# Summing each window of nodes in PSUM, with the bank named by a register, in a four-layer graph network kernel

## The reference

```
# layer 0, twice (a and b): 4 bases, 8 edge types
m   = sum_b comp[etypes][:, b, None] * (h @ basis[b])[src] * norm[:, None]
agg = segment_sum(m, dst);  out = agg + bias + h @ loop_w
# layer 1: 8 bases, 32 edge types, the same without loop_w
# layer 2: deg = number of edges of dst, at least 1
ah  = segment_sum(x[src], dst) / deg[:, None];  out = x @ W1.T + b1 + ah @ W2.T + b2
# layer 3: attention over the same edges, 4 blocks of 4 heads
```

## Time and profile before

| | |
|---|---|
| median of 3 runs | 3148.48 us (3147.07 to 3153.4) |
| the profiled execution | 3150.06 us; its span 3148.7 us |
| L0a: steps, then turn | 47.65 to 326.8, then to 346.0 us |
| transform of L0a | to about 501 us |
| L0b: steps with turns | 514.1 to about 778 us (rows landed at 505.5) |
| L1: steps with turns | 906.8 to about 1203 us |
| layer 2 up to layer 3 | 1439 to about 1535 us |
| busy over the span | PE 94%, DVE 66%, ACT 40%, POOL 37% |

### The profile page before, as it was taken

How to read it: one execution, slowest core, us unless ns; L and a number is a source line. 1 busy time by engine, 2 the same in 40 slices (tenths; PEclk the granted TensorE clock), 3 DMA queues, 4 the chain that set the end, 5 groups by cost and what they waited for, 6 DMA issues and landing times.

```text
span 3148.7 us, 43883 instructions
## 1 busy us (share of the span) xinstructions
PE 2973.9 (94%) x14658; PEld 2178.0 (69%) x14658; DVE 2078.8 (66%) x5077; ACT 1274.5 (40%) x2245; POOL 1175.2 (37%) x938
## 2 busy tenths in 40 slices
PE   6899998999979899999999999999999999999999
PEld 3333775445843357875458998789987999779987
DVE  6999324886358853345377678567766776767777
ACT  4666531002340033342264454345543555435554
POOL 4666336665456643342012123511135101431022
PEclk8999999999989999999999999999999999999999
DMA  2555534555246643333013001210013001130012
GB/s 79 164 165 163 165 97 134 170 170 152 74 126 178 178 114 94 96 99 127 10 43 91 14 31 50 97 48 8 31 56 124 14 8 64 44 103 15 8 64 80
DMA packets 129600, 279.37 MB, mean 89 GB/s; under 512 B 22743, under 2 KB 45591, under 8 KB 128355
## 3 DMA queue, kind: packets, MB, share of 16 engines
q0 software_dynamic: 40320, 132.15, 14.6%
q1 hardware_dynamic: 87618, 141.76, 14.2%
q10 hardware_dynamic: 1440, 2.62, 0.2%
HBM read 227.85 MB, written 27.48 MB: 81 GB/s over the span
## 4 chain that ended last, share of the span: by engine, by line
PE 74%; DVE 12%; issue 9%; ACT 2%; DMA 2%; POOL 1%; DVEq 0%; another core or an unknown queue 0%; SPq 0%; POOLq 0%; ACTq 0%
PE bank L162 16%; PE bank L163 15%; PE bank L164 15%; PE bank L893 11%; PE bank L2548 5%; PE bank L2212 3%; PE bank L1853 2%; PE bank L861 2%; DVE y_tile L2164 1%; DVE y_tile L2166 1%; DVE columns L2147 1%; DVE G L1000 1%; DVE onehot_dst L967 1%; PE bank L907 1%; DMA yT_lo<-yT_new_lo 1%
## 5 line engine op out<-in xcount | busy, mean ns | idle before, releaser
L893 PE MATMUL bank<-gathered,selector 128*128 x1328 | 650.8, 614 | 57.6 <-SPq L849 32.0
L1000 DVE TENSOR_TENSOR G<-G,bank 128x512 f32 x664 | 453.7, 683 | 20.5 <-PE bank L893 20.0
L893 PEld LDWEIGHTS bank<-gathered,selector 128*128 128x128 f32 x1328 | 233.8, 194 | 312.8 <-issue 176.3
L2636 ACT CAST probT<-bank 128x512 fp32r<-128x512 f32 (+2 forms) x480 | 212.1, 516 | 261.8 <-PE bank L2548 260.9
L1514 POOL TENSOR_TENSOR weight_parts<-weight_ring,weight_parts 128x512 fp32r<-128x512 f32 x130 | 187.7, 1444 | 294.1 <-ACT weight_parts L1447 294.0
L2718 DVE CUSTOM_DVE_ANT_0 prob<-bank,count_by_src 128x512 f32<-128x512 f32 (+1 forms) x480 | 258.3, 588 | 58.8 <-PE bank L164 58.8
L1473 DVE TENSOR_TENSOR lhs_parts<-G,lhs_parts 128x640 fp32r<-128x640 f32 x122 | 102.3, 839 | 285.4 <-ACT lhs_parts L1445 285.2
L2644 DVE TENSOR_TENSOR probT<-bank,probT 128x512 fp32r<-128x512 f32 (+2 forms) x480 | 254.2, 585 | 50.8 <-ACT probT L2636 50.2
L871 ACT COPY G<-bank 128x512 f32<-128x512 f32 x160 | 82.4, 659 | 496.2 <-issue 250.7
L162 PE MATMUL bank<-weight_parts,lhs_parts 128*128 128x512 f32 x680 | 267.4, 393 | 11.1 <-POOL weight_parts L1514 5.6
L164 PE MATMUL bank<-weight_parts,lhs_parts 128*128 128x512 f32 x680 | 265.4, 390 | 0.0
(11 more groups left out here) (293 smaller groups left out, 6813.5 us busy)
## 6 DMA issues: line engine op xcount, KB each, us to landing
weight_ring<-in_L_gnn_basis SPq DMA_DIRECT2D x64, 256.0 KB, 2.6
weight_ring<-in_L_gnn_bases SPq DMA_DIRECT2D x64, 256.0 KB, 2.6
x_L<-x_rows SPq DMA_DIRECT2D x50, 256.0 KB, 4.3
x_rows<-x_L SPq DMA_DIRECT2D x50, 256.0 KB, 5.5
yT_hi<-yT_new_hi SPq DMA_DIRECT2D x4, 2560.0 KB, 11.3
yT_lo<-yT_new_lo SPq DMA_DIRECT2D x4, 2560.0 KB
count_rows<-count SPq DMA_DIRECT2D x10, 642.0 KB, 5.5
count_by_dst<-count_rows SPq DMA_DIRECT2D x10, 642.0 KB, 4.4
```

The costliest lines, as they stand in the source:

```text
L893: ins = pe.matmul(bank[s % banks][:], sel[:, s % SELECTORS, :], tile_rows_of[s % BATCH], start=True, stop=True)
L1000: ins = dve.tensor_tensor(g, g, bank[s % banks][:], ALU.add)
L2636: ins = act.copy(hi, of)
```

## The change

**In the steps.** A window now has a PSUM bank of its own, number (w + 1) % 4 for window w, and TensorE adds up all the window's steps in it (`start=False`), the bank named by a register. ScalarE clears four banks at the start; then, for each window, it waits for the window's last step (its number is in a new table, `end_of_window`), copies the bank into G once and clears it for the window four further on. VectorE only makes selectors; before each it waits until the bank of the step's window is cleared. G isn't cleared any more, and has no row for dropped steps. TensorE's register batch has twelve values, and more addresses.

**Counting.** Each step has one bf16 product of two one-hots, 128 rows (4 * node + high) by 320 (low), which adds up in banks 4 to 7 in the same way. VectorE makes both one-hots (L939, fp16 to bf16). ScalarE copies and clears 320 columns more for each window. The signs, PATHC and the halving go; layer 2 sums a row of counts (`sum_row`) for the degree where it formed the difference, and a row load now waits for that sum and for TensorE's transposes of the row four before.

**Around them.** Takes between steps are VectorE's; those behind the last step are ScalarE's and VectorE's in turn. The memset before L0b and L1 and the clearing at the start are gone. The setup makes `end_of_window`, bank numbers and the split of `src` and `dst` numbers in place of PATHC's tables.

The core of the diff (`aggregate`):

```diff
     def on_pool():
-        if free:
-            for token in free:
-                pool.wait_ge(*token)
-            pool.memset(G[:, 0:cleared, :], 0.0).then_inc(*zeroed_pool.inc())
         if counting:
             for t in range(RING):
                 gather(t)
         for token in ready:
             pool.wait_ge(*token)
-        if counting:
-            for first in range(0, counting.first, CLEARED):
-                pool.memset(G[:, first:min(first + CLEARED, counting.first), :], 0.0).then_inc(*zeroed_pool.inc())
...
     def on_pe():
         for token in ready:
             pe.wait_ge(*token)
-        tile_rows_of, tiles = batch(0)
+        tiles, rows_of, sums, counts = batch(0)
         for s in range(steps):
+            pe.wait_ge(*selected(s + 1))
+            if counting:
+                pe.matmul(counts[s % BATCH], counting.rows[:, s % SELECTORS, :], counting.sources[:, s % SELECTORS, :],
+                          start=False, stop=False, skip_group_check=True)
             pe.wait_ge(tiles_landed.semaphore.sem, tiles[s % BATCH])
-            pe.wait_ge(*selected(s + 1))
-            ins = pe.matmul(bank[s % banks][:], sel[:, s % SELECTORS, :], tile_rows_of[s % BATCH], start=True, stop=True)
-            if s >= banks:
-                ins._wait_ge(*added(s - banks + 1))
-            ins.then_inc(*multiplied.inc())
+            pe.matmul(sums[s % BATCH], sel[:, s % SELECTORS, :], rows_of[s % BATCH], start=False, stop=False,
+                      skip_group_check=True).then_inc(*multiplied.inc())
...
+        for w in range(windows):
+            b = sum_bank(w)
+            if w % BATCH == 0:
+                over = [v & COUNTED for v in table(C.end_of_window[path][0:1, w:w + BATCH], ACTE, 1, steps)]
+            act.wait_ge(multiplied.semaphore.sem, over[w % BATCH])
+            act.copy(G[:, w, :], psum[:, b, :]).then_inc(*summed.inc())
+            if counting:
+                act.copy(counting.count[:, w, :], psum[:, SUM_BANKS + b, 0:LOW]).then_inc(*counted.inc())
+            if w + SUM_BANKS < windows:
+                act.wait_ge(*summed(w + 1))
+                ins = act.copy(psum[:, b, :], C.zero[:].to_broadcast([P, D]))
+                if counting:
+                    act.wait_ge(*counted(w + 1))
+                    ins = act.copy(psum[:, SUM_BANKS + b, 0:LOW], C.zero[:].to_broadcast([P, LOW]))
+                ins.then_inc(*cleared.inc())
+        for n in range(NT * KC):
+            if taker[n] is act:
+                take(n, act)
+
+    def select(s, window):
+        at = s % SELECTORS
+        if s >= SELECTORS:
+            dve.wait_ge(*multiplied(s - SELECTORS + 1))
         if counting:
+            for onehot, numbers, place in ((counting.rows, counting.numbers[:, 0:P], C.row_in_window),
+                                           (counting.sources, counting.numbers[:], C.src_low)):
+                dve.tensor_scalar(onehot[:, at, :], numbers, place[:, s:s + 1], None, ALU.is_equal)
+        dve.wait_ge(cleared.semaphore.sem, window)
         dve.scalar_tensor_tensor(
...
     def on_dve():
...
-            g = sums[s % BATCH]
-            ins = dve.tensor_tensor(g, g, bank[s % banks][:], ALU.add)
-            if s:
-                ins._wait_ge(*added(s))
-            ins.then_inc(*added.inc())
...
-                dve.wait_ge(*multiplied(s + 2))
-            if s + AHEAD < steps:
-                select(s + AHEAD)
...
+        for s in range(steps + AHEAD):
+            if s < steps:
+                if s % BATCH == 0:
+                    begun = [v & COUNTED for v in table(C.window_of_step[path][0:1, s:s + BATCH], DVE, 1, windows)]
+                select(s, begun[s % BATCH])
+            if s >= AHEAD:
+                for work in beside:
+                    work.beside_on_dve(s - AHEAD)
+                if turns_after(s - AHEAD) is not None:
+                    for k in range(KC):
+                        take(turns_after(s - AHEAD) * KC + k, dve)
+        for j in late:
+            for n in range(j * KC, (j + 1) * KC):
+                if taker[n] is dve:
+                    take(n, dve)
```

In layer 2:

```diff
     def load_row(j):
         if j >= ROWS:
-            sp.wait_ge(*differed(j - ROWS + 1))
-            sp.wait_ge(*topped(j - ROWS + 1))
+            sp.wait_ge(*summed(j - ROWS + 1))
+            sp.wait_ge(*turned(GROUPS * (j - ROWS + 1)))
```

520 lines of the change are left out of this document (203 added, 317 removed).

## The result

The changed kernel took 3120.23 us (median of 4 runs, 3114.9 to 3126.27), the kernel before beside it 3150.94 (3147.07 to 3158.14): a ratio of 0.990, 95% interval 0.9874 to 0.9927. The profiled execution took 3121.2 us where that of before took 3150.06: -29 us. The forecast was -69 (3080), and the result lies 2 us above the range's end of 3118; rival 1 had 3114.

The account below looks back on a forecast made before the run. VectorE was taken to pace L0a and TensorE L0b, with no engine full in L1. The terms -47 -6 -3.5 -21 +3 +4.4 +1.3 = -69 us gave about 3080 us, range 3042 to 3118.

Parts of the forecast that it names:

- rival 1: GpSimd's gathers and their pauses bind, not VectorE: L0a -29, L0b -3, L1 -8, in all -35, 3114 us; chance 0.19.
- The step that failed: L0a priced at TensorE's 209 us times 1.11, 232 us; L1's gathers at 1.26 us each, 212 us.
- My signs of being wrong: L0a's gathers over 1.1 us on the mean, TensorE idle for "issue" every fourth step, or products waiting for selectors.
- L0a's terms: First aggregation: VectorE's adds and count work go, TensorE's count products shrink, steps take 232 us: -47 us.
- L0b: Second aggregation's steps: waits for adds go, but TensorE is busy all but 8.7 us: -6 us (0 to -12).
- Its start: L0b's start: without GpSimd's memset the first product comes at about 510.4, not 514.1: -3.5 us (0 to -4.5).
- L1: Third aggregation: waits for VectorE's add go and the gather is late next: -21 us, bounds -6 and -38.
- ScalarE's copies cost nothing: ScalarE's window copies in L0a (106 us in all at most) and L1 were costed at nothing.
- Registers: TensorE's longer register batches in all three aggregations, covered by its queue of issued products: +3 us, bounds 0 and 78 to 115.
- rival 3: Ports: each of 416 one-hots in L0a waits for a running gather: +292 us, about 3372 us; chance 0.04.
- Around the steps: Takes and turns: +2.3 us in L0a, +0.6 in L0b, +1.5 in L1, together +4.4.
- Layer 2: Layer 2 reduces one count row where it subtracted two, and TensorE bounds it: 0 us.

Follow-up runs that it names:

- e8_takes_both: The changed kernel with the takes between steps by ScalarE instead of VectorE in L1 and L0b, on chip 7: 3037.22 us, ratio 0.9818.
- e3_ring16: The changed kernel with 16 places for gathered tiles instead of 8: 3136.96 us, ratio 0.9959.
- e5_direct: The changed kernel with direct loads of consecutive rows by SyncE in place of GpSimd's gathers, on chip 7: 3035.06 us.
- e4_takes_act: The changed kernel with the takes between the steps of L1 by ScalarE instead of VectorE: 3115.88 us, ratio 0.9904.
- e14_takes_both: The changed kernel with the takes between steps by ScalarE in L1 and L0b, on chip 15: 3130.36 us, ratio 0.9902.
- e2_load_twice: The changed kernel with TensorE's register load of each batch done twice: 3120.04 us, ratio 0.9915.
- e11_direct_again: The changed kernel with direct loads by SyncE in place of GpSimd's gathers, on chip 3: 3036.25 us.
- e13_filler: The changed kernel with a memset of 340 columns by GpSimd after each gather, on chip 15: 3130.24 us, one run.
- e16_more_events: The changed kernel with 16 more semaphore increments by SyncE per tile, on chip 15: 3353.25 us, one run.
- e6_short_rows: The changed kernel with gathers of 512 bytes a row instead of 2048 and products over 128 columns, on chip 7: 2976.29 us.

## Why the prediction was wrong

**The step that failed** is the pricing of L0a and L1: "The two engines near 205 us will not meet their floor ... I take 1.11", and for L1 "what is late next is the gather: 168 x 1.26 = 212 us". Both price GpSimd at its fastest period, 1.26 us, and L0a then as TensorE's floor of 209 us times 1.11; measured it is 1.20 times that floor. What GpSimd keeps up here is 1.48 to 1.49 us: 160 x 1.49 = 238 us, and some 12 us of filling and of the last tiles make the 251 measured. Given that pace, L1 could gain next to nothing, where I had -21. The number was to be had blind: 128 gathers in 189 us of L1 before, shown above. It did not lie where rival 1 saw it: the "27.7 us of 160 for nothing visible" are 75 waits of 0.37 us, little more than the usual 0.30. And I read GpSimd's 23.7 us of waits for a place as proof that it was not first. In the changed kernel, between 100 and 240 us, such waits are 23 with 22.7 us, pauses among them; where nothing pauses (e8_takes_both) they are 34 with 10.4 us, 0.3 each. So most of what is booked as a wait for a place is the pause itself, and twice as many places did not end it (e3_ring16). Rival 1, at 0.19, is what happened: L0a -26 for its -29, L0b with its start -7 for -6.5, L1 0 for -8, 3120 for its 3114.

My signs of being wrong did not show it either. The gathers of L0a took 960 ns on the mean (the sign was 1.1 us), TensorE's idle time for "issue" before a count product came 15 times and not in each of 52 batches, and products waited 6.1 us for selectors. The sign that was missing is GpSimd's period from start to start; the length of a gather says nothing of it.

- *L0a's terms.* The one-hots took 305 and 285 ns where I had 0.41 and 0.21 us at most: 0.59 us a step for 0.62, right in sum, though the smaller one is above its bound. VectorE fell far under TensorE (140 us busy to 224), where I had it just under. TensorE at 224 of 251 us is 89% busy, in the forecast "over 85%", and shows that a busy share near the top does not mean that an engine binds. Its base of 0.99 us a step is right: in e5_direct twenty steps take 19.9 us.
- *L0b* -5.5 for -6. Its start -1.6 for -3.5: the clearing and the selectors were done in time, but the first tile landed late, 6.6 us from the first gather (480.09 us) to the first product (486.73) where before it was 3.4.
- *L1* 0 for -21. TensorE's waits for VectorE's add are gone between 890 and 1050 us, as forecast, and 6 us with them in the first 180 steps; the rest was already GpSimd's. The last 68 steps gave the 6 us back. TensorE waits there for the takes, which are VectorE's now (L865, 684 ns), and at no time for a selector. The waits of the changed kernel between 1060 and 1170 us:

```profile
DVE selector L941 <- ACT banks L923: 19.7, 12, 3.4
DVE G L865 <- PE banks L854: 15.2, 11, 5.7
PEld banks L854 <- DVE G L865: 13.3, 12, 3.7
PE banks L854 <- DVE G L865: 10.2, 10, 3.5
```

  Before, TensorE's transposes waited 8.5 us there for ScalarE's takes, so VectorE's takes explain 2 us at most. The 68 steps took 110.7 us with TensorE busy for 98.1 at a granted clock of 0.95, where before they took 104.8 with 95.2 at 0.98: 3 us of the 6 are longer busy time at a lower clock, 3 are idle time. In e4_takes_act they took 104.9, with 93.6 busy at a clock of 1.00; the idle time, 11.3 us, is nearly that of the changed kernel (12.6). So most of what that trace won is the clock, and the times of e4_takes_act and e14_takes_both confirm no gain. That VectorE's takes cost the 6 us is therefore not shown.
- *ScalarE's copies cost nothing*, right: they took 586 ns, and in L1 VectorE waits for a cleared bank (44.3 us in 25 times between 890 and 1050), while TensorE waits 3.0 us there for a selector.
- *Registers* +3, and the idea of the cover was right: e2_load_twice shows none of it exposed, and in e11_direct_again TensorE is busy 180.00 of 180 us with all the register work in it. So the term is nearer to 0. The sequencers' loads in L0a, by engine (min/median/max ns):

```profile
L808 DVEq TENSOR_LOAD <-window_of_step x51: 337/342/346, 48.2 to 279.9; - x51
L808 PEldq TENSOR_LOAD <-registers_by_step x50: 382/848/857, 50.1 to 286.1; - x50
```

  Twelve values take 848 ns, for 0.84 estimated.
- *Ports (rival 3)*, wrong: beside 416 one-hots the gathers of L0a took 960 ns. By the Trainium skill, page "SBUF — State Buffer", section "Who interferes with whom", two-port work of VectorE would hold GpSimd back. The trace does not show it here: between 100 and 240 us the gathers are shorter than before the change (1057 ns on the mean and up to 1412 then, 960 and up to 1045 now).
- *Around the steps.* L0a's turn went from 20.5 to 20.7 us and not up by 2.3, which is partly luck: TensorE does wait 1.9 us for VectorE's first operands (L1403), as forecast, but the 1.4 us that the turn waited for VectorE's last count sum (L975) before are gone. L1's end +2.2 for +1.5. *Layer 2* 0, right.

## What to carry to other kernels

Take an engine's pace from a long stretch, start to start, with everything between, in a stage where it may already bind; its best period is a floor that was kept on one chip of the four here. When one engine frees up and the next one shows idle time for "issue" or for a releaser that is on no record, count its operations per microsecond before calling it idle, and look whether all engines resume at one instant. Compare a kernel with the one before on the same chip: one and the same program took from 3094 to 3160 us on them. And before a trace's 6 us are put down to an edit, look at the granted clock in both.

## What was not expected of the hardware

1. **The pauses are not on every chip.** The kernel before: 3148.71, 3150.63, 3160.36 and 3149.88 us on chips 14, 3, 15 and 15, and 3093.99 on chip 7; with SyncE's direct loads in place of gathers 3036.25 on chip 3 and 3035.06 on chip 7. Chip 7 was used for one group alone, so whether it is the chip or its state at that time is not shown; chip 15 itself gave 3160 and 3150.

2. **Where engines pause, the trace lacks events.** SyncE waits for each landed tile. Its waits between 100 and 240 us, first in the changed kernel (94 gathers), then in e8_takes_both on chip 7 (111 gathers):

```profile
SPq L834 <- DMA gathered<-in_x,src_index: 41.3, 27, 3.7
```

```profile
SPq L837 <- DMA gathered<-in_x,src_index: 136.4, 110, 3.0
```

   Counted over the whole trace, semaphore increments are 17903 in the changed kernel and 24483 in e8_takes_both, whose program differs only in who makes the takes; of the 16 DMA increments of a gather a quarter is there between 100 and 240 us (354 of 1504). e13_filler, without long pauses, has 23610, e11_direct_again 24485. So pauses and lost records go together, and with SyncE's 8064 more events the pauses are longer (from one gather's start to the next up to 6.7 us between 100 and 240 us in e16_more_events, and up to 4.1 in the changed kernel). That fits a shared path that events or their records go through and that holds all sequencers when it is full. The Trainium skill, page "NOTIFIC — the notification-queue block", section "7.1 Overflow: three behaviours, one of which stalls the engine", describes a path of that kind for the records, whose internal pipeline pushes back rather than lose a record and could in that way throttle an engine. That it does so here is argued and not shown, and records are missing here all the same. No run separates the events from their recording: the executions that were only timed agree with the profiled one (3120.2 and 3121.2 us), but for them too a span and a granted clock were recorded. So whether a kernel that nobody records would pause **stays open**, as does why GpSimd's gathers bring it about and SyncE's loads, with as many increments, don't.

3. **A gather's length doesn't depend on its bytes**: 966 ns with 512 bytes a row (e6_short_rows), 968 with 2048 (e8_takes_both), both on chip 7.
